# A bidirectional state-space layer: the next unit's side chain, and the side stages behind it, in other slots

## What is computed

```
xz = in_proj_w @ xn                      # x half and z half, 256 channels each
for each direction (forward; backward on the reversed sequence):
    u     = silu(conv4(x) + conv_b)                    # causal, 4 taps, per channel
    x_dbl = x_proj @ u                                 # 8 rows for delta, 16 for B, 16 for C
    delta = softplus(dt_proj @ x_dbl[:8] + dt_bias)
    h[l]  = exp(delta*A) * h[l-1] + delta * B * u      # 256 channels x 16 states
    y     = (sum over states of h * C + D * u) * silu(z)
mamba = out_proj @ (y_forward + y_backward)
ffn   = quantize4(xn @ Hadamard) @ ternary(weight)
```

## Time and profile before

| | us |
|---|---|
| median of three runs | 961.72 (961.13 to 965.54) |
| profiled execution | 959.55 |
| its span, first to last instruction | 957.4 |
| mean granted TensorE clock | 0.887 of full |

### The profile page before, as it was taken

How to read it: one execution, slowest core, us unless ns; L and a number is a source line. 1 busy time by engine, 2 the same in 40 slices (tenths; PEclk the granted TensorE clock), 3 DMA queues, 4 the chain that set the end, 5 groups by cost and what they waited for, 6 DMA issues and landing times.

```text
span 957.4 us, 13831 instructions
## 1 busy us (share of the span) xinstructions
PE 779.1 (81%) x3873; PEld 386.4 (40%) x3873; DVE 800.7 (84%) x838; ACT 781.2 (82%) x1454; POOL 750.3 (78%) x454
## 2 busy tenths in 40 slices
PE   3587986979888896988879798796988789698885
PEld 1233443443534444333354444343353343444352
DVE  2278887899888878898898888788988998998994
ACT  2499995899969898699968999489995999779970
POOL 2159888788878978699887888868886898778994
PEclk9789988889887889899988999788988999898796
DMA  3434326070430606125070512506044070703400
GB/s 89 105 77 102 64 63 128 4 164 4 118 81 13 154 3 154 46 57 107 18 182 3 130 37 71 126 3 161 6 104 93 3 164 3 175 15 78 87 14 20
DMA packets 50857, 72.44 MB, mean 76 GB/s; under 512 B 6144, under 2 KB 19344, under 8 KB 50832
## 3 DMA queue, kind: packets, MB, share of 16 engines
q1 hardware_dynamic: 50400, 71.87, 32.3%
q10 hardware_dynamic: 432, 0.26, 0.1%
HBM read 60.58 MB, written 11.53 MB: 75 GB/s over the span
## 4 chain that ended last, share of the span: by engine, by line
POOL 26%; issue 22%; ACT 22%; PE 19%; DVE 8%; DMA 1%; POOLq 1%; ACTq 0%; DVEq 0%; SPq 0%
POOL hst L678 20%; ACT da L415 8%; PE pb L792 7%; ACT dbx_t L404 6%; DVE hst L569 5%; POOL dbx_t L688 3%; PE b_ps L879 3%; PE b_ps L864 3%; PE y L896 2%; POOL t_log L694 2%; PE pb L811 1%; PE pb L819 1%; PE pb L799 1%; DVE pb L523 1%; ACT xn L307 1%
## 5 line engine op out<-in xcount | busy, mean ns | idle before, releaser
L678 POOL TENSOR_TENSOR hst<-hst,c_rep 128x1024 f32<-128x1024 f32 x256 | 600.3, 2364 | 152.9 <-DVE hst L569 146.9
L569 DVE TENSOR_TENSOR_SCAN hst<-da,b_ps 128x512 f32<-128x512 f32 x512 | 584.6, 1201 | 31.5 <-PE b_ps L879 14.4
L879 PE MATMUL b_ps<-ident,dbx_t 128*128 128x128 f32 x1536 | 257.6, 308 | 129.3 <-DVE hst L569 127.7
L415 ACT ACTIVATE da<-rep,neg_a 128x511 f32<-128x511 f32 x512 | 335.1, 709 | 2.8 <-DMA rep<-d_scr 1.8
L879 PEld LDWEIGHTS b_ps<-ident,dbx_t 128*128 128x128 f32 x1536 | 187.4, 155 | 291.0 <-DVE hst L569 270.1
L404 ACT ACTIVATE dbx_t<-du_t,b_t 128x256 f32<-128x256 f32 x576 | 246.9, 495 | 2.5 <-PE b_ps L879 1.7
L896 PE MATMUL y<-hst,sum_sel 128*32 128x512 f32 x1024 | 162.6, 713 | 2.4 <-POOL hst L678 2.4
L792 PE MATMUL pb<-xnt,conv_wt 128*128 128x512 f32 x256 | 122.5, 624 | 0.8 <-ACT xnt L315 0.8
L688 POOL TENSOR_TENSOR dbx_t<-du_t,b_t 128x1024 f32<-128x1024 f32 x48 | 91.3, 1902 | 2.7 <-ACT du_t L387 2.7
L557 DVE TENSOR_TENSOR b_ps<-b_ps,b_rep 128x1024 f32<-128x1024 f32 x64 | 78.1, 1220 | 6.5 <-PE b_ps L864 6.5
L864 PE MATMUL b_ps<-t_log,spread_sel 32*128 32x512 f32 x256 | 70.2, 687 | 14.4 <-POOL t_log L740 9.0
(11 more groups left out here) (111 smaller groups left out, 581.5 us busy)
## 6 DMA issues: line engine op xcount, KB each, us to landing
rep<-d_scr SPq DMA_DIRECT2D x128, 256.0 KB, 9.2
c_rep<-bc_scr SPq DMA_DIRECT2D x64, 256.0 KB, 4.9
d_scr<-t_pos SPq DMA_DIRECT2D x15, 512.0 KB, 2.9
b_rep<-bc_scr SPq DMA_DIRECT2D x64, 64.0 KB, 2.4
x_ln<-x SPq DMA_DIRECT2D x8, 256.0 KB, 3.1
x_res<-x SPq DMA_DIRECT2D x8, 256.0 KB, 2.7
out<-x_res SPq DMA_DIRECT2D x8, 256.0 KB, 9.4
conv_wt<-conv_w SPq DMA_DIRECT2D x2, 512.0 KB, 5.9
```

The costliest lines, as they stand in the source:

```text
L415: nc.scalar.activation(da[s % 2][:, j, 1:L], rep[d][h][:, j, 1:L], ACT.Exp, scale=neg_a[:, d, h, j, q:q + 1]).then_inc(decay_done, 1)
L569: nc.vector.tensor_tensor_scan(hst[s % RING][:, j, :], da[s % 2][:, j, :], b_ps[:, j, :], 0.0, ALU.mult, ALU.add).then_inc(scan_done, 1)
L678: nc.gpsimd.tensor_tensor(hst[s % RING][:, two, :], hst[s % RING][:, two, :], c_rep[d][:, q:q + 1, :].broadcast_to([P, 2, L]), ALU.mult).t ...
L879: ins = tr(b_ps[:, j, P * c:P * (c + 1)], dbx_t[(NX * d + q - 1) % 2][:, c, NJ * h + j, :, :].rearrange("p r e -> p (r e)"), ident[:, :])
```

## The change

No operation is added or taken away; b_transposed writes the other bank of pb, and one wait is added on SyncE. In each engine's list side stages move to other slots or halves of slots:

- conv of half 0 goes to the middle of slot 6, of half 1 to the middle of slot 7; make_u of half 0 to the end of slot 7, of half 1 to the middle of slot 0;
- x_proj goes to the middle of slot 0, both steps to its end; log1p to the middle of slot 2, delta to its end;
- transpose_xq, b_transposed and hadamard join skip_products in the middle of slot 3; z_proj goes to the end of slot 3, project to slot 4;
- du_transposed stands at the ends of slots 5 and 6, transpose_xn in the middle of slot 5, ahead of the second half of the transposes;
- gates go to the end of slot 4, token_max to the end of slot 3, quantize to the end of slot 5; the small stages of ScalarE and GpSimd are moved to match.

```diff
--- before.py
+++ after.py
@@ -221,6 +221,7 @@
                 for r in range(NR):
...
                                  bc_scr[d][r:r + 1, :].broadcast_to([CB, L])).then_inc(b_loaded[d], DMA)
+                wait(sp, sum_done, SLOTS * (V - 1))
                 by_r = bc_scr[d][NS:2 * NS, :].rearrange("(q r) l -> r q l", r=NR)
...
                     sp.dma_start(c_rep[d][CB * r:CB * (r + 1), :, :],
@@ -339,7 +340,7 @@
             def keep_bt(d, V):
...
                 wait(act, bm_pool, NX * (V - 1))
-                nc.scalar.activation(b_t[d][:, :, :], pb[:, 0, 0:NC * NS].rearrange("p (c n) -> p c n", c=NC), ACT.Copy).then_inc(bt_ready, 1)
+                nc.scalar.activation(b_t[d][:, :, :], pb[:, 1, 0:NC * NS].rearrange("p (c n) -> p c n", c=NC), ACT.Copy).then_inc(bt_ready, 1)
 
...
                 wait(act, u_ready, 2 * V + 2)
@@ -430,6 +431,7 @@
             keep_dut(0, 0, 0)
...
             inputs_t(0, 0, 1, 0)
+            inputs_t(0, 0, 1, 1)
 
...
                 U = 2 * b + d
@@ -439,56 +441,60 @@
                 for s in range(SLOTS):
...
                     if s == 0:
-                        if d == 0 and not first(b):
+                        if nxt:
+                            u_sigmoid(e, V, 0)
+                        if d == 1 or not first(b):
                             keep_dut(d, U, 1)
-                        inputs_t(d, U, 1, 1)
                     if s == 1:
...
                     if s == 2:
+                        inputs_t(d, U, 2, 1)
                         if nxt:
                             keep_xdbl(e, V)
+                    if s == 3:
+                        if nxt:
+                            softplus_log(V)
+                        if d == 0 and not last(b):
+                            log_var(b + 1)
+                        inputs_t(d, U, 2, 2)
+                    if s == 4:
+                        inputs_t(d, U, 3, 0)
                         if d == 0 and not first(b):
                             keep_xqt(b - 1)
-                        inputs_t(d, U, 2, 2)
                         if nxt:
                             keep_bt(e, V)
-                    if s == 3 and nxt:
-                        softplus_log(V)
-                        if d == 0 and not last(b):
-                            log_var(b + 1)
-                    if s in (4, 5):
-                        inputs_t(d, U, 3, 2 * (s - 4))
+                    if s == 5:
+                        if d == 0:
+                            z_sigmoid(b)
+                        inputs_t(d, U, 3, 2)
                     if s == 6 and d == 0 and not last(b):
                         normalize(b + 1)
-                    if s == 7 and d == 0:
-                        if not last(b):
-                            keep_xnt(b + 1)
+                    if s == 7 and nxt:
                         keep_dut(e, V, 0)
+                        inputs_t(e, V, 1, 0)
                     decays(b, d, s, 1)
...
                         inputs_t(d, U, 1, 2)
-                        if nxt:
-                            u_sigmoid(e, V, 0)
                     if s == 1:
                         inputs_t(d, U, 2, 0)
-                        inputs_t(d, U, 2, 1)
-                    if s == 2:
+                    if s == 2 and nxt:
+                        softplus_in(e, V)
+                    if s == 3:
+                        if d == 0 and not last(b):
+                            guess_rstd(b + 1)
                         inputs_t(d, U, 2, 3)
-                        if nxt:
-                            softplus_in(e, V)
-                    if s == 3 and d == 0 and not last(b):
-                        guess_rstd(b + 1)
-                    if s in (4, 5):
-                        inputs_t(d, U, 3, 2 * (s - 4) + 1)
-                    if s == 5 and d == 0:
-                        z_sigmoid(b)
-                    if s == 6 and d == 0:
-                        keep_longer(b)
+                    if s == 4:
+                        inputs_t(d, U, 3, 1)
+                    if s == 5:
+                        inputs_t(d, U, 3, 3)
+                        if d == 0:
+                            keep_longer(b)
+                    if s == 6 and d == 0 and not last(b):
+                        keep_xnt(b + 1)
                     if s == 7 and nxt:
-                        keep_dut(e, V, 1 - d)
-                        inputs_t(e, V, 1, 0)
+                        inputs_t(e, V, 1, 1)
 
...
                 unit(b, 0)
@@ -630,31 +636,32 @@
                 for s in range(SLOTS):
...
                     if s == 0 and nxt:
-                        make_u(e, V, 0)
+                        if d == 0 and first(b):
+                            make_u(e, V, 0)
+                        make_u(e, V, 1)
                     if s == 1 and d == 0 and not first(b):
                         gate_y(b - 1, 1)
-                    if s == 3 and nxt:
+                    if s == 2 and nxt:
                         log1p(V)
-                    if s == 5:
-                        if d == 0:
-                            gates(b, 0)
-                            gates(b, 1)
-                        else:
-                            token_max(b)
-                    if s == 6 and d == 1:
-                        quantize(b)
-                    scan(b, d, s, 1)
-                    if s == 0:
-                        if nxt:
-                            make_u(e, V, 1)
-                        if d == 0 and not first(b):
-                            gate_y(b - 1, 0)
-                    if s == 1 and d == 0 and not last(b):
-                        statistics(b + 1)
-                    if s == 3 and nxt:
-                        delta(V)
                     if s == 5 and d == 1 and not first(b):
                         add_residual(b - 1, pb[:, 1, :])
+                    scan(b, d, s, 1)
+                    if s == 0 and d == 0:
+                        if not first(b):
+                            gate_y(b - 1, 0)
+                        if not last(b):
+                            statistics(b + 1)
+                    if s == 2 and nxt:
+                        delta(V)
+                    if s == 3 and d == 1:
+                        token_max(b)
+                    if s == 4 and d == 0:
+                        gates(b, 0)
+                        gates(b, 1)
+                    if s == 5 and d == 1:
+                        quantize(b)
+                    if s == 7 and not last(b):
+                        make_u(d, U + 2, 0)
 
...
                 unit(b, 0)
@@ -761,15 +768,15 @@
                     if s == 7 and nxt:
...
                         inputs_t(e, 1)
-                    if s == 5 and d == 1:
+                    if s == 4 and d == 1:
                         max_known(b)
                     states_times_c(b, d, s, 1)
-                    if s == 5 and d == 1:
+                    if s == 4 and d == 1:
                         scales(b)
                     if d == 0 and not last(b):
-                        if s == 1:
+                        if s == 0:
                             moments(b + 1)
-                        if s == 4:
+                        if s == 3:
                             refine(b + 1)
...
             def body(b):
@@ -803,7 +810,7 @@
                 pe.wait_ge(xdbl_ready, V + 1)
...
                 for c in range(NC):
-                    ins = mm(pb[:, 0, NS * c:NS * (c + 1)], xdbl[d][0:XC, P * c:P * (c + 1)], ident[0:XC, DR:DR + NS], start=True, stop=True)
+                    ins = mm(pb[:, 1, NS * c:NS * (c + 1)], xdbl[d][0:XC, P * c:P * (c + 1)], ident[0:XC, DR:DR + NS], start=True, stop=True)
                 ins.then_inc(bt_filled, 1)
...
             def steps(d, h, free, count):
@@ -937,57 +944,58 @@
 
...
                     next_inputs(s, 0)
-                    if s == 1 and nxt:
+                    if s == 0 and nxt:
+                        x_proj(e, V)
+                    if s == 3:
                         if d == 0 and not first(b):
-                            b_transposed(e, V, xqt_ready, b)
+                            transpose_xq(b - 1, delta_ready, V + 1)
+                        if nxt:
+                            b_transposed(e, V, delta_ready, V + 1)
+                        if d == 1:
+                            if nxt:
+                                hadamard(b, delta_ready, V + 1)
+                            else:
+                                hadamard(b, dut_ready, 2 * U + 2)
+                        skip_products(b, d)
+                    if s == 4 and d == 1 and not first(b):
+                        if nxt:
+                            project(b - 1, (0, 1), bt_ready, V + 1)
                         else:
-                            b_transposed(e, V, u_ready, 2 * V + 2)
-                        steps(e, 1, xdbl_ready, V + 1)
-                    if s == SKIP_AT:
-                        skip_products(b, d)
-                    if s == 4:
```

(59 more changed lines are left out.)

## The result

| | before | after |
|---|---|---|
| median of 9 runs, us | 963.21 (961.13 to 966.0) | 955.17 (953.82 to 960.36) |
| profiled execution, its span | 959.55, 957.4 | 957.31, 955.2 |
| mean granted TensorE clock | 0.887 | 0.874 |

The nine runs of before don't contain its profiled execution. The ratio of the times is 0.9921, with a 95% interval of 0.9901 to 0.9941: the change makes the kernel 0.8% faster. The forecast was 960, 0.2% faster than the 961.72 shown then, with 941 to 982 as its range.

The account below looks back on a forecast made before the run. No engine is full, so order decides, through VectorE's stalls. Span 957.4 + 6 x (113.1 - 113.4) - 1 = 954.6, with 2.15 around it 956.8; the median, 2.2 above, 959, stated as 960, range 941 to 982.

Parts of the forecast that it names:

- The logarithm: log1p in slot 2: VectorE stalls 0 forward, 0.8 backward, a gain of 3.1 us a batch; waits for Ln under 8.
- Slot 3 on TensorE: Side work gathered in slot 3: stalls 0.1 forward, 0.5 backward; add_residual finds project 1.1 late, its waits 8 or more.
- The scale: quantize at slot 5's end, its scale at slot 4's: 0.1 us of stall where 1.5 was, gain 1.4.
- The convolution: Halves in slots 6 and 7: VectorE waits 0.5 us for transposes after slot 6, and 1.4 for u in each unit.
- The forward unit: transpose_xn waits for normalize: transposes 0.45 us late, the next 0.2, and a stall of 2.35 in slot 7.
- The clock: TensorE's lower clock behind gaps at log1p, quantization and transpose_xn costs 3.0 us a batch; bounds 0 and 9.
- SP: The wait for sum_done ahead of the c_rep loads costs nothing, at most 1.9 us of queued issues, hidden.
- The ends: First batch changes by 0; last batch by -1 us, its logarithm's stall of some 1.6 going.
- A: Rival: denser TensorE work stays at 2.4 GHz, batch 110.1, kernel 941 us; chance 0.29.
- B: Rival: the first convolution half runs at the lower clock in both units, batch 117.5, kernel 984 us; chance 0.18.
- C: Rival: ScalarE, held in slot 4, makes decays late in slots 5 and 6, 1.5 more a unit, 978 us; chance 0.11.

Follow-up runs that it names:

- experiment 7: The changed kernel with quantize back in the middle of slot 6, token_max and its scale staying early: 932.71 us, ratio 0.967 to the kernel before.
- experiment 10: The kernel before with token_max and the scale a half slot earlier, and quantize moved to the end of slot 5: 955.31 us, ratio 0.9893.
- experiment 9: Experiment 7's kernel with the forward units' first convolution half behind slot 7's second transposes: 943.36 us, ratio 0.9781.
- experiment 11: Experiment 7's kernel with two quarters of inputs_t ahead of the waiting copies in ScalarE's slot 4: 918.09 us, ratio 0.9514.
- experiment 12: The changed kernel, quantize at slot 5's end, with two quarters of inputs_t ahead of the waiting copies in ScalarE's slot 4: 942.62 us, ratio 0.9781.
- experiment 2: The changed kernel with token_max half a slot later, in the middle of slot 4: 954.81 us, ratio 0.9898.
- experiment 3: The changed kernel with transpose_xn behind slot 6's second transposes, as before the change: 954.41 us, ratio 0.9885.
- experiment 4: The changed kernel with keep_longer on ScalarE behind normalize and the decays instead of ahead of them: 955.09 us, ratio 0.9903.
- Experiment 5: The changed kernel with two matmuls by zeros added in the middle of slot 2 of every unit: 957.45 us, ratio 0.9934.
- experiment 6: The changed kernel with skip_products of backward units in the middle of slot 2 instead of slot 3: 957.35 us, ratio 0.9925.
- experiment 1: The changed kernel with the first unit's second make_u half and one inputs_t quarter put back as before: 957.99 us, ratio 0.9918.

## Why the prediction was right, point by point

The sign was right and the time within 5 us; the main mechanism, stalls moved from the logarithm and the scale to TensorE, is what the traces show. The size was not: 1.7 us of gain were forecast and the medians give 8.0. That the span of the profile (955.2) meets the forecast sum (954.6) is luck: -5.1 instead of -1.8 in the steady batches, +4.7 instead of 0 in the first, -3.5 instead of -1 in the last, and 1.7 ahead of them that has nothing to do with the change. Within a batch the balance was good: 13.9 us of stalls and clock forecast, 12.9 of stalls measured in the batch above. By the prediction's parts:

1. **The logarithm.** Forward units 0, as forecast. Backward units 1.0 to 1.8 instead of 0.8. The two go with steps on TensorE: it takes 3.6 us in the backward units whose logarithm is 1.75 late (at 571.54, below), and 1.98 in those where it is 0.99 late. The working took full clock there. In all 10.6, where under 8 was forecast: this sign was missed.
2. **Slot 3 on TensorE.** 1.65 to 1.73 before token_max instead of 0.5: the transposes and the sums ahead of hadamard ran at the lower clock, b_transposed in part (1.23 us against 1.06; the rows under "hardware" below). add_residual waits 0.79 instead of 1.1. Ahead of its last wait add_residual rose from 3.8 to 5.1 in all, where the sign asked for 8 or more: missed.
3. **The scale.** Its stall is gone in all steady batches; the gain is right. Here the step failed that cost the change most: it priced only quantize's wait for its operand, and not what quantize covers. The place in slot 6, 3.2 us of VectorE beside 3.6 us of TensorE, was given away for it; experiments 7 and 10 put 22 us on that in the new order and 3 in the old (with the reserve on the scale said there). The prediction's part 4 reckoned 3.63 of convolution against 3.4 that fit, and noted no cover that it could have.
4. **The convolution.** The stall at slot 7's second scans in backward units is 0.2 in five steady batches and 1.2 in one (0.5 forecast); u's wait is 1.22 to 1.65 in each unit against 1.4; TensorE runs without gap from the first half to the second (553.6 to 564.2). Right for the change; that the order of this work doesn't matter, experiment 9 refutes (10.6 us).
5. **The forward unit.** Forecast 0.45 + 0.2 + 2.35 = 3.0, measured 0.32 + 1.98 = 2.3, in two of six units 1.70 more. Right in mechanism: with ScalarE's wait filled, experiments 11 and 12 gain 12 to 15 us. Not seen: y_gated's wait for the sums, 0.8 to 0.9 in four of the six steady forward units, those whose steps took 2.9 us on TensorE instead of 1.98.
6. **The clock.** Its toll was put on the first convolution halves, and in this profile it wasn't there: they take 3.60 us, the price at full clock, but for one in each of the first two batches (4.28 and 4.18). In the profiles of experiments 2 to 6, which differ from the change by one small move each, it is there in most backward units. So the part was right on where the risk lay; one profile tells it for one execution. The lower level stood at steps and, behind the gap at log1p (4.19 us in the unit shown below), in slot 3, which the working had as over "before the side stages begin". The 3.0 us a batch of the forecast came out as 0.9 more at the logarithm in four of the six steady batches and 1.1 at amax. Experiment 5 filled one gap: 0.03 more of clock and no time, as the lower level stayed behind the next gap.
7. **SP.** Right: c_rep's loads are issued straight behind b_rep's (536.09, and b_rep's at 533.81 for 2.17 us).
8. **The ends.** The first batch was mis-sized, 4.7 slower instead of 0. VectorE's stalls in its two units are 24.8 against 20.3: u 6.27 for 3.03 + 0.91, the first decays 5.75 for 4.72, and four waits of 4.6 us from slot 5 on (before 1.6, with the gate's), less 1.65 at the logarithm. Only the first of these was in the working, and the gains set against it came mostly in backward units. The last batch gave 3.5 instead of 1.

**The rivals.** A (the clock stays up, 941) did not come: the mean clock fell. B (the first convolution half at 1.2 GHz in both units, 984) did not come: 3.60 us in both units of the steady batches but one (4.18). Its mechanism is real in backward units, by experiments 2 to 6, at 1 to 2 us each. C (late decays, 978): VectorE waited for decays once, 5.7 us in the first unit. None of the three held the interplay of quantize and the first convolution half.

What stays open: of the 8.0 us between the medians the profiled executions show only 2.2, and no experiment tells which part of the remaining 5.8 belongs to which stall. And the intervals of experiments 1 to 6 all overlap the change's, so it is shown that they give little, not that they give nothing. Each trace is one execution, up to 6.5 us off its kernel's median (experiment 12), so waits and medians are compared with that reserve.

## What to carry to other kernels

Before moving a long side stage for its own wait's sake, look at what it covers: an engine's long stage belongs beside the long stage of the engine that it waits for, here quantize over the convolution (22 us, with the gap that it left and the clock behind it). Where an in-order engine waits for a copy's source, put independent work that is due soon ahead of it (12 to 15 us for two moved operations). And test each part of a many-part change alone: the scale's half-slot move alone gave more than the whole change, and quantize's move hid what the rest was worth.
